# State-space chunks: rows of summed decays fetched by transfers instead of a TensorE sum, the drop formed on ScalarE, y in two PSUM banks

## The reference, cut to what matters

```
adt = a * dt;  g = exp(adt);  lam = sigmoid(trap)
def step(h, bx_prev):                      # for each token t
    bx = x_t (outer) B_t
    h  = g_t*h + dt_t*(lam_t*bx + (1-lam_t)*g_t*bx_prev)
    y_t = h . C_t
y = (y + D*x) * silu(z);   out = y @ W_out.T
```

## Time and profile before

| | us |
|---|---|
| median of 3 runs | 2175.49 (2172.94 to 2176.54) |
| the profiled execution's own time | 2173.8 |
| its span in the trace | 2172.0 |
| PE busy | 1866.3 (86%) |
| DVE busy | 1787.1 (82%) |
| ACT busy | 1378.2 (63%) |
| POOL busy | 1295.0 (60%) |

### The profile page before, as it was taken

How to read it: one execution, slowest core, us unless ns; L and a number is a source line. 1 busy time by engine, 2 the same in 40 slices (tenths; PEclk the granted TensorE clock), 3 DMA queues, 4 the chain that set the end, 5 groups by cost and what they waited for, 6 DMA issues and landing times. The chain is left out here.

```text
span 2172.0 us, 32672 instructions
## 1 busy us (share of the span) xinstructions
PE 1866.3 (86%) x10276; PEld 993.4 (46%) x10276; DVE 1787.1 (82%) x2181; ACT 1378.2 (63%) x2602; POOL 1295.0 (60%) x954
## 2 busy tenths in 40 slices
PE   5898989887989898779888499996689999999987
PEld 5333333333333333234565278884234555565532
DVE  6599899999898999978877899996977666667683
ACT  3666666767676767448335477773167877777776
POOL 4789899999898999952134255544662111111276
PEclk7999999999989999899998799996589999999999
DMA  3345454455445455532003000001334334333212
GB/s 81 110 154 153 148 155 158 155 157 160 147 153 153 154 153 155 160 104 71 31 1 95 0 1 0 0 0 59 93 87 121 94 111 118 99 112 111 74 39 79
DMA packets 156310, 217.53 MB, mean 100 GB/s; under 512 B 31722, under 2 KB 68603, under 8 KB 155547
## 3 DMA queue, kind: packets, MB, share of 16 engines
q1 hardware_dynamic: 152074, 207.41, 31.5%
q0 software_dynamic: 4096, 8.40, 1.5%
HBM read 196.59 MB, written 23.86 MB: 101 GB/s over the span
## 5 line engine op out<-in xcount | busy, mean ns | idle before, releaser
L1035 POOL TENSOR_TENSOR m_dBx<-m_du,m_rowB 128x1024 f32<-128x1024 f32 x256 | 605.0, 2389 | 4.7 <-DMA m_rowB<-bc_rows 4.5
L758 PE MATMUL ps<-m_hC,ident 128*128 128x512 f32 x1024 | 512.8, 647 | 99.2 <-DVE m_hC L1117 99.2
L3225 DVE TENSOR_REDUCE a_mx<-ps 128x2 f32<-128x1024 f32 (+2 forms) x320 | 344.6, 1114 | 100.7 <-PE ps L2799 55.8
L934 ACT ACTIVATE ps<-m_delta,m_A 128x512 f32<-128x512 f32 x512 | 332.7, 682 | 143.7 <-DVE m_hC L1117 112.8
L3017 ACT ACTIVATE a_pT<-ps 128x512 f32<-128x512 f32 (+2 forms) x640 | 318.0, 563 | 135.0 <-PE ps L2827 116.9
L758 PEld LDWEIGHTS ps<-m_hC,ident 128*128 128x128 f32 x1024 | 203.6, 206 | 391.8 <-issue 231.4
L3381 POOL TENSOR_SCALAR_AFFINE_SELECT a_pT<-a_pT 128x512 f32<-128x512 f32 x104 | 66.0, 637 | 372.0 <-ACT a_pT L3017 370.6
L1117 DVE TENSOR_TENSOR m_hC<-ps,m_rowC 128x1024 f32<-128x1024 f32 x176 | 215.3, 1223 | 16.7 <-issue 1.3
L1108 DVE TENSOR_TENSOR_SCAN ps<-ps,m_dBx 128x1024 f32<-128x1024 f32 x88 | 201.1, 2285 | 33.3 <-ACT ps L934 16.7
L1045 POOL TENSOR_TENSOR m_hC<-m_h,m_rowC 128x1024 f32<-128x1024 f32 x80 | 194.6, 2432 | 45.5 <-DVE m_h L1108 45.3
L1108 DVE TENSOR_TENSOR_SCAN ps<-ps,m_carry,m_dBx 128x1024 f32<-128x1024 f32 x88 | 206.3, 2345 | 5.5 <-ACT m_dBx L959 4.6
(11 more groups left out here) (410 smaller groups left out, 3618.6 us busy)
## 6 DMA issues: line engine op xcount, KB each, us to landing
m_rowB<-bc_rows SPq DMA_DIRECT2D x256, 256.0 KB, 4.0
m_rowC<-bc_rows SPq DMA_DIRECT2D x256, 256.0 KB, 3.4
a_w<-in_L3f_w1T SPq DMA_DIRECT2D x39, 256.0 KB, 2.7
a_w<-in_L3f_w2T SPq DMA_DIRECT2D x39, 256.0 KB, 3.8
expert_rows<-in_zero_rows SPq DMA_DIRECT2D x39, 128.0 KB, 2.6
a_xs<-expert_rows SPq DMA_DIRECT2D x39, 128.0 KB, 2.6
expert_out<-a_y SPq DMA_DIRECT2D x39, 128.0 KB, 3.6
qk_parts<-a_part SPq DMA_DIRECT2D x18, 256.0 KB
```

The lines of the kernel that those rows point to most:

```text
L758: mm = pe.matmul(ps[:, bankY + c, :], k.ident[:], hC[:, n % NBUF, c, :], start=False, stop=n % NS == NS - 1)
L934: act.activation(decays(n)[:, c, :], delta[:, i % 2, c, chunk(i, x)], ACT.Exp, scale=An[:, ITEMS[i][0], c, s:s + 1]).then_inc(decayed, 1)
L1035: pool.tensor_tensor(dBx[:, n % NBUF], du[:, i % 2, :, chunk(i, x)], rowB[:, n % 4, :].unsqueeze(1).to_broadcast([P, HALF, CH]), ALU.mult) ...
L3225: dve.tensor_reduce(mx[:, c % 2, :, es[0]:es[0] + len(es), t, x // CH], src, AX_X, ALU.max)\
```

## The change

`cum` of all chunks is turned once in the gates stage (a PE transposition and an ACT copy) and stored in DRAM as 128 rows. In the chunk stage SP fetches for each chunk the rows of its four heads, 512 numbers, onto all 128 partitions, into two buffers in turn. ACT takes `ebc` from there; it forms `drop` = relu(cum_s - cum_t), 0 where s > t, and E = exp(-drop) in one wide operation. The mask moves into the weights: `strict` holds a large negative number where s > t, and wt = max(strict*v + wdiag, 0), with v kept at 1e-25 or more. The product L2206, the four `ta` pieces and the four `arg` operations go. y takes two banks, one for two heads each, so that both D products stand ahead of the eight narrow ones. ACT, PE, DVE and POOL have another order within a step. The load of the mask goes.

```diff
@@ gates stage
+                when(sp, A, "rows")
+                sp.dma_start(L["cum_rows"], turned[:]).then_inc(L["cum_stored"], 16)
...
+                T.done(pe.transpose(k.ps[0:NT * H2, 4, 2 * P:3 * P], flat(L["cum"][:]), k.ident[:]), "turn")
...
+                when(act, T, "turn")
+                when(act, V, "v")
+                A.done(act.copy(turned[:], k.ps[0:NT * H2, 4, 2 * P:3 * P]), "rows")
...
-                when(dve, T, "shift")
-                step(dve.tensor_copy(L["v"][:], small(k.ps[:, 4, 0:NT * H2])), "v")
+                when(dve, T, "turn")
+                step(dve.tensor_scalar(L["v"][:], small(k.ps[:, 4, 0:NT * H2]), LOW, None, ALU.max), "v")
@@ chunk stage, SP
+            def _(sp):
+                sp.wait_ge(L["cum_stored"], 16)
+                for c in range(NT):
+                    if c >= 2:
+                        when(sp, SA, "drop", c - 2)
+                    src = L["cum_rows"][c * H2:(c + 1) * H2, :].rearrange("h t -> (h t)")
+                    sp.dma_start(flat(rows[:, c % 2]), src.partition_broadcast(P)).then_inc(s_row[c % 2], 16)
@@ DVE: argument() goes; cFe stands ahead of g and H
-                        argument(r, u)
+                    if s is not None:
+                        when(dve, SA, "cF", s)
+                        when(dve, RA, "ebc", s)
+                        when(dve, BT, "y", s - 2)
+                        SV.done(dve.tensor_tensor(flat(cFe[:, 1 - u]), k.ps[:, trC, :], flat(ebc[:, 1 - u]), ALU.mult), "cFe")
@@ POOL: xw (s) stands ahead of Ht (b)
@@ ACT
-                        for hd in range(H2):
-                            t = act.activation(ta[:, hd, :], k.triu[:], ACT.Copy, scale=L["adt"][:, ds(r, 1), hd])
+                        act.wait_ge(*row_loaded(r, u))
+                        when(act, SV, "cFe", r - 2)
+                        RA.done(act.activation(flat(ebc[:, u]), flat(rows[:, u]), ACT.Exp), "ebc")
+                    if s is not None:
+                        act.wait_ge(*row_loaded(s, 1 - u))
+                        when(act, SA, "E", s - 1)
+                        for hd in range(H2):
+                            t = act.activation(drop[:, hd, :], rows[:, 1 - u, hd, :], ACT.Relu, scale=-1.0,
+                                               bias=L["cum"][:, ds(s, 1), hd])
+                        SA.done(t, "drop")
...
-                        SA.done(act.activation(E[:, 1 - u], arg[:], ACT.Exp), "E")
+                        SA.done(act.activation(flat(E[:, 1 - u]), flat(drop[:]), ACT.Exp, scale=-1.0), "E")
...
-                            t = act.activation(wt[:, 1 - u, hd, :], L["strict"][:], ACT.Identity,
+                            t = act.activation(wt[:, 1 - u, hd, :], L["strict"][:], ACT.Relu,
@@ PE
-                        RT.done(pe.matmul(k.ps[:, cum, :], k.ones[:], flat(ta[:]), start=True, stop=True), "cum")
...
+                        for q in range(2):
+                            pe.matmul(k.ps[:, yb + q, 0:P], flat(L["winD"][:, 2 * q:2 * q + 2, :]),
+                                      xns[:, u, :], start=True, stop=False, skip_group_check=True)
+                        y = lambda hd: k.ps[HP * (hd % 2):HP * (hd % 2) + HP, yb + hd // 2, 0:P]
                         when(pe, SV, "M", b)
                         for hd in range(H2):
+                            pe.matmul(y(hd), xs[:, u, hd * HP:hd * HP + HP], M[:, u, hd, :], start=False, stop=False,
+                                      skip_group_check=True)
+                        for hd in range(H2):
+                            t = pe.matmul(y(hd), H[:, hd, :], cFe[:, u, hd, :], start=False, stop=True, skip_group_check=True)
```

More of the change, by code:

```diff
@@ L1762, in mamba3_gates_stage @@
         A = Steps(k, "act", ["wabs", *of("sq", "std")[:2 * early], *(f"sm{n}" for n in range(4)), "exp", "ln", "etrap",
-                             *of("sq")[early:2 * early], *(f"z{n}" for n in range(2 * NCH)), "eend", "ewb",
+                             *of("sq")[early:2 * early], *(f"z{n}" for n in range(2 * NCH)), "eend", "rows", "ewb",
                              *[x for u in range(early, groups) for x in ([f"std{u}"] if u < 2 * early else [f"sq{u}", f"std{u}"])],
@@ L1766, in mamba3_gates_stage @@
         T = Steps(k, "pe", ["wsum", *of("x")[:early], *(f"sm{n}" for n in range(4)), *of("x")[early:2 * early],
-                            *(f"z{n}" for n in range(2 * NCH)), "cum", "end", "shift", *of("x")[2 * early:],
+                            *(f"z{n}" for n in range(2 * NCH)), "cum", "end", "shift", "turn", *of("x")[2 * early:],
                             *(f"th{c}" for c in range(CPB))])
@@ L1837, in _ @@
                         when(pe, V, "wb")
+                        when(pe, A, "rows")
                     if c in (2, 4):
@@ L2020, in mamba3_chunks_stage @@
         xs, xns = sb("x", [P, 2, DI2]), sb("xn", [P, 2, P])
-        ta = sb("triu_adt", [P, H2, P])
+        rows, drop = sb("cum_rows", [P, 2, H2, P]), sb("cum_drop", [P, H2, P])
         bch = sb("bch", [P, 2, 2, H2, P])
@@ L2026, in mamba3_chunks_stage @@
         bF, cF, cFe = sb("bF", [P, H2, P]), sb("cF", [P, H2, P]), sb("cFe", [P, 2, H2, P])
-        ebc, arg, E = sb("ebc", [P, 2, H2, P]), sb("arg", [P, H2, P]), sb("E", [P, 2, H2, P])
+        ebc, E = sb("ebc", [P, 2, H2, P]), sb("E", [P, 2, H2, P])
         M = sb("M", [P, 2, H2, P])
@@ L2038, in mamba3_chunks_stage, with row_loaded @@
         zero = k.sem("s_H_zero")
-        trB, trC, cum, st, yb, xb, outb, stateb = range(8)
+        s_row = [k.sem(f"c2_row{x}") for x in range(2)]
+        trB, trC, st, xb, outb, stateb, yb = range(7)
+        def row_loaded(c, u):
+            return s_row[u], c * 8 + (16 - 8 * u)
         def pipeline(step, eng):
@@ L2054, in mamba3_chunks_stage @@
         with nc.Block() as block:
+            @block.sync
+            def _(sp):
[5 more added lines that the diff above has]
+                    sp.dma_start(flat(rows[:, c % 2]), src.partition_broadcast(P)).then_inc(s_row[c % 2], 16)
+                for x in range(2):
+                    sp.wait_ge(s_row[x], 16 * NT // 2)
             @block.vector
@@ L2134, in step @@
                     wide = lambda x, c: x[:, ds(c, 1), :].rearrange("p a h -> p (a h)").unsqueeze(2).to_broadcast([P, H2, HP])
+                    if s is not None:
+                        when(pool, SA, "x", s)
+                        when(pool, BT, "state", s - 2)
+                        hold(k, pool)
+                        x = xs[:, 1 - u, :].rearrange("p (h n) -> p h n", h=H2)
+                        SG.done(pool.tensor_tensor(xw[:, 1 - u], x, wide(L["wb"], s), ALU.mult), "xw")
                     if b is not None:
@@ L2181, in step @@
                                                scale=L["v"][:, ds(s, 1), hd], bias=L["wdiag"][:, ds(s, 1), hd])
                         SA.done(t, "wt")
[L2183 to L2193, removed]
@@ L2198, in _ @@
             def _(pe):
-                for stream in (RT, ST, BT):
+                for stream in (ST, BT):
                     stream.seed(pe)
                 def step(r, s, b, u):
-                    if r is not None:
-                        when(pe, RA, "ta", r)
-                        when(pe, RV, "arg", r - 1)
-                        RT.done(pe.matmul(k.ps[:, cum, :], k.ones[:], flat(ta[:]), start=True, stop=True), "cum")
                     if b is not None:
@@ L2236, in step @@
+                        for hd in range(H2):
+                            t = pe.matmul(y(hd), H[:, hd, :], cFe[:, u, hd, :], start=False, stop=True, skip_group_check=True)
                         BT.done(t, "y")
                     if s is not None:
-                        when(pe, SA, "cF", s)
+                        when(pe, SA, "bF", s)
                         when(pe, SV, "Q", s - 1)
```

78 lines of the change are left out of this document (31 added, 47 removed).

## The result

| | before | after |
|---|---|---|
| median, us (9 runs each) | 2176.54 (2170.65 to 2185.33) | 2163.15 (2155.47 to 2167.40) |
| ratio after / before | | 0.9931 [0.9908, 0.9954] |
| profiled execution's own time | 2173.8 | 2164.1 |
| stage, from the clearing of H to the last addition | 222.1 | 206.6 |
| between state products, full steps | 6.634 | 6.256 |

The kernel is faster by 13.4 us (the ratio's interval is 10 to 20 us). The forecast was 2139.7 with a range of 2134 to 2156: the sign is right, the size is not, and the time lies outside the range. The stage lasted 15.6 us less where 36.2 had been forecast (32.5 + 2.5 + 1.2). In the two profiled executions the spans differ by 9.7 only, since the first product of L1230, in another layer ahead of the stage, starts 4.8 us later in the one of after (970.2 and 975.0), in code that the change doesn't touch.

A forecast was written before the change was run, and what follows sets the result against it. PE's stream was to bind at 5.43 us a step, 5.55 with 0.12 for jitter: 30 steps save 32.5 us, the ends 3.3, together 35.8. From 2173.8 that gives 2138.0, plus 1.7 for the median 2139.7, range 2134 to 2156.

The forecast's parts named there:

- PE's sum: PE's step: 6.64 less 0.86 for L2206 and 0.35 for the y block's saved width change, 5.43 us.
- the DVE term, "6.49 - 1.12 = 5.37": DVE's step: busy time 6.49 less 1.12 for the four `arg` operations, giving 5.37 us.
- PE's own stream sets the step, with DVE 0.14 us behind it: Kernel before: PE's products follow without a hole for 6.64 us a step and bound it, DVE 0.14 us behind.
- POOL's `xw` ahead of `Ht` costs nothing: 3.49 of 5.55 busy: POOL's new order within a step was to cost nothing, POOL being busy 3.49 of 5.55 us.
- Rival 1: DVE and POOL become the bound, POOL's rope pieces blocking n1 and M: step 5.9 us, 2150.3; chance 0.15.
- DVE's ladder: Forecast order within a step: DVE has 0.3 to 0.4 us of waiting for the scores, where a stall hides.
- Rival 5: Narrow products keep their price and DVE's stall hides the rest: step 5.78 us or over, 2146.6; chance 0.08.
- ACT and the transfers: ACT's step 5.23 us with `drop` at 1.28; row landing 3.2, making a two-buffer ring of 5.2 us a step.
- rivals 2 and 3: Row ring binds: landing 4.0, step 6.0, 2153.3, chance 0.13; or landing 4.9, step 6.9, 2180.2, 0.05 shared with rival 4.
- The 2.6: Row landing in us by the skill's fit for another queue, ring an estimated 4.6; the forecast took 3.2 instead.
- Rival 4: PE streams with holes and its clock falls below 1.00: kernel over 70 us slower; chance 0.05 shared with rival 3.
- The ends: Outside the full steps: fill gains 2.5 us, drain 1.2, gates stage loses 0.4, together 3.3.

The follow-up runs named there:

- e_all2: Changed kernel with POOL's `Ht` ahead of `xw`, and DVE's `Q` and `pa` results left in PSUM for M and `n1`: 2133.51 us, ratio to before 0.9809.
- e_ht_first: Changed kernel with POOL's old order, `Ht` ahead of `xw`: 2156.8 us, stage 200.5.
- e_m_psum_g_first: Changed kernel with `Q` left in PSUM for M, POOL's `Ht` ahead of `xw`, and DVE's `g` and `H` ahead of `cFe`: 2138.9 us, stage 190.0.
- e_m_psum: Changed kernel with `Q` left in PSUM, so that M has one SBUF input only: 2163.8 us, stage 207.5.
- e_y_order: Changed kernel with PE's y products in the old order by halves, two banks kept: 2167.0 us, step 6.25.

## Why the prediction was wrong in size

- **PE's sum was right.** 6.64 - .86 - .35 = 5.43: y block 1.56 measured for 1.57, and e_all2 runs at 5.43 with no hole between PE's starts. (The old block's halves were not equal as the prediction has it, but .91 and 1.01; its sum uses their 1.92 and is right.) It just was not what bound the changed kernel.
- **The step that failed is the DVE term, "6.49 - 1.12 = 5.37".** Two errors, the second the large one. First, 6.49 is busy time. DVE's stream before was full at the spacing of 6.63, since between `bch` and `pa` it must wait for itself (starts 1.36 apart for 1.21 of work). Taking off the 1.04 that `arg` occupied leaves 5.59, above PE's 5.43 already, but only .04 above the 5.55 of the forecast: 1.2 us in 30 steps. So "PE's own stream sets the step, with DVE 0.14 us behind it" was not shown either; both streams were full before, and no run tells which of them set the step. Secondly I took DVE's other durations as fixed. In after `xw` stands under `pa` (+.38), `Ht` under `pb` (+.41) and a POOL rope piece under all of `n1` (+.28), while M was freed (-.42). That is +.65: 5.59 + .65 = 6.24, measured 6.23.
- **What brought these pairs together was only in part the new order.** `Ht` went from M to `pb` by POOL's order: e_ht_first moves it back. `xw` waits for ACT's copy of x in every kernel. The copy begins 2.20 us behind the state product now and 3.14 before, since ACT makes it earlier in its step, and `xw` follows at 2.89 and 3.84; with POOL's old order it still meets `pa` (.60 in e_ht_first). `n1` lasts .86 with either order undone and .85 with both undone (e_m_psum_g_first), so neither of the two brought its partner. DVE comes to it 2.81 us behind the start of `pb` now and 3.43 before, when `arg` stood between them. That the missing `arg` is the reason is argued from this; no run put it back.
- **"POOL's `xw` ahead of `Ht` costs nothing: 3.49 of 5.55 busy" was wrong.** POOL did have room. The price was on DVE: with POOL's old order the step is .19 and the stage 6.1 us shorter.
- **Rival 1 was the right mechanism, with the wrong size and place.** It had a chance of .15, 5.9 us and the places n1 and M; it was 6.24, at n1, `pa` and `pb`. What I held against it, .3 to .4 us of waiting in DVE's ladder, did not exist: the ladder was made of PE's and ACT's times, and DVE's own was never laid out. The Trainium skill (SBUF — State Buffer, Who interferes with whom) says that a DVE operation with two SBUF inputs contends with a GpSimd one that reads SBUF, and that this is an exclusive lock. The runs agree in every pair: `pa` .43 and .80, `pb` .42 and .83, `n1` .41 and .86, M .68 and 1.10, each without and with such a partner. How much a pair costs depends on how far the two overlap (`pa` with `xw`: .80 in after, .60 in e_ht_first), so the rule alone would have named the pairs but not the time; for that their starts had to be laid out.
- **Rival 5 falls**: the narrow products did become cheaper. That its step of 5.78 or over came about is rival 1's work, and by it the removed product is worth .20 of .86 in this kernel.
- **ACT and the transfers were right.** Four `drop` pieces take 1.26 (1.28 taken), ACT is busy 5.30 a step (5.23 taken). Landing is 3.3 (3.2 taken), never waited for after the first; so rivals 2 and 3 fall. The 2.6 that the Trainium skill's fit gave (DMA: Bandwidth & Descriptors, anatomy of one DMA on the gpsimd path) is for another queue, and SP's did not show it: the least was 3.0.
- **Rival 4 falls.** The clock stayed at 1.00 with 0.44 us of holes in a step. In the fill it was 0.50, the 1.2 GHz level, and the fill still gained 2.7 (2.5 taken).
- **The ends were right**: 2.7 and 1.5 for 2.5 and 1.2, and 0.3 for the gates' 0.4.

So of the 20.6 us that the stage missed (36.2 forecast, 15.6 measured) nothing was lost in transfers or clock: 30 x (6.256 - 5.55) = 21.2 is DVE's stream, and the ends gave 0.5 back. The median missed the forecast by 23.4; the other 3 us or so lie outside the stage, and no run explains them. e_all2 recovers the stage's loss: it is 38.5 shorter than that of before. There PE sets the step again, so that by PE's sum both of its savings, .86 and .35, count in full.

## What to carry to other kernels

An engine's busy sum minus what is removed is not its new sum: lay out its stream by starts, and for each DVE operation with two SBUF inputs look up which POOL operation will stand beside it, even where POOL has room. Not only a new order moves the pairs: an earlier copy (x) and a shorter stretch between two operations do so too. Where an operation lasts much longer than its equal in the same trace, look for a wait that no idle column shows. A change of order moved the collision on here (steps of 6.04 to 6.06); one operand in PSUM took it away (5.43).

## What the runs showed of the hardware

- A DVE operation of 128x256 with both inputs in SBUF takes .41 to .43 alone and .80 to .86 beside a POOL operation, and 128x512 .68 and 1.10; with one input in PSUM it takes the same .41 and .68 with POOL beside it. In the trace the wait is part of the duration, and in the full steps no idle time is put down to POOL.
- It acts the other way too, and the one that starts first keeps its own length. In after `xw` starts .10 ahead of `pa`: .61 and .80. In e_all2 `pb` starts .01 ahead of `xw`: .42, and .89 for `xw`. POOL's `Ht` took .61 in e_all2 (beside M with a PSUM input) and .79 in after, where it starts while `pa` still runs.
- Reading and writing the same PSUM bank cost DVE next to nothing: Q took .68 in e_m_psum and .70 in e_all2, .68 before.
- Going a second time from products of full width to those of 64 columns and back costs TensorE .36 us: the block that does so twice took 1.92 (before) and 1.93 (e_y_order, with two banks too), that with one such change 1.56, with the same passes. The change between the M and the H products, also made once more, is in this and was not taken apart.
- Rows of 2 KB spread over 128 partitions, 256 KB in all, landed 3.0 to 3.4 us after their issue on SP's queue in the full steps, with no other transfer of this kernel beside them, and 3.7 at most in the fill, where two run at once.
